# A mixture of experts' last sum: rows stored by token, one more choice on TensorE, shared tiles moved behind the experts, and a first wait for two gathers

## The reference

```python
# x: (T=2048, H=256), E=64 experts, M=176, K=6 choices, C=96 places per expert, MS=352
scores = softmax(x @ gate_weight.T)                  # group-limited, then
topk_w, topk_i = top_k(masked scores, 6)
pos  = running count of the choice's expert          # over all tokens and choices
slot = topk_i * C + minimum(pos, C - 1)              # overflow shares the last place
buf[slot] = x[token]                                 # (E, C, H)
out = (silu(buf @ Wg.T) * (buf @ Wu.T)) @ Wd.T       # per expert
y   = sum over k of out[slot[t, k]] * topk_w[t, k]
shared = (silu(x @ Sg.T) * (x @ Su.T)) @ Sd.T
result = residual + y + shared
```

## Time and profile before

| | |
|---|---|
| median of 3 runs | 1515.64 us (1514.18 to 1516.43) |
| profiled execution | 1511.05 us |
| its span | 1509.4 us |
| mean granted TensorE clock | 0.963 |
| busy: PE / DVE / ACT / POOL | 1376.7 / 1053.4 / 820.4 / 356.5 us |
| DMA moved | 215.08 MB |

### The profile page before, as it was taken

The page is one execution under the profiler, slowest core; times in us unless marked ns, Lnnn a source line. Parts: engine busy times, 40 slices in busy tenths (PEclk is TensorE's granted clock), DMA queues, the critical chain, the costliest instruction groups (busy, mean ns, idle before and its releaser), DMA issues. The chain is left out here.

```text
span 1509.4 us, 36481 instructions
## 1 busy us (share of the span) xinstructions
PE 1376.7 (91%) x12868; PEld 969.4 (64%) x12869; DVE 1053.4 (70%) x2256; ACT 820.4 (54%) x1701; POOL 356.5 (24%) x782
## 2 busy tenths in 40 slices
PE   5769999998779999999979999999997989899977
PEld 3435455454656777777767677777775945799953
DVE  7866777773878888888831888888887679322228
ACT  2335566565138778777820777877785155122230
POOL 0145656420111011111110111110102000677730
PEclk9969999999889999999999999999999999999985
DMA  3059898850027767676640676666666050799958
GB/s 105 1 140 217 247 250 231 217 125 22 1 81 137 138 135 142 136 139 135 133 77 1 111 138 134 137 133 136 132 135 134 29 167 1 217 280 287 272 158 289
DMA packets 463449, 215.08 MB, mean 142 GB/s; under 512 B 412130, under 2 KB 434496, under 8 KB 463120
## 3 DMA queue, kind: packets, MB, share of 16 engines
q1 hardware_dynamic: 449040, 175.09, 51.6%
q0 software_dynamic: 12000, 36.90, 8.2%
q10 hardware_dynamic: 2336, 2.16, 0.4%
HBM read 81.97 MB, written 31.52 MB: 75 GB/s over the span
## 5 line engine op out<-in xcount | busy, mean ns | idle before, releaser
L1076 PE MATMUL bank<-a_pt,v_part 128*128 128x128 f16 x3456 | 234.2, 219 | 17.3 <-DMA a_pt<-a_ph 12.7
L1139 ACT ACTIVATE a_ph<-a_p,a_rinv 128x1024 f16<-128x1024 f32 (+7 forms) x256 | 198.7, 777 | 80.6 <-POOL a_rinv L1018 75.3
L758 DVE TENSOR_REDUCE a_qh<-bank 128x1 f16<-128x1024 f32 (+7 forms) x256 | 182.3, 755 | 84.3 <-PE bank L648 81.8
L1076 PEld LDWEIGHTS bank<-a_pt,v_part 128*128 128x128 f16 x3456 | 207.6, 98 | 51.1 <-DMA a_pt<-a_ph 10.2
L1147 DVE TENSOR_REDUCE a_negm<-bank 128x1 f32<-128x1024 f32 (+7 forms) x256 | 191.8, 750 | 57.0 <-PE bank L1060 56.8
L1055 PE MATMUL bank<-a_k,a_q 128*128 128x512 f16 (+3 forms) x1152 | 228.6, 326 | 0.2
L746 ACT ACTIVATE a_p<-bank 128x1024 f32<-128x1024 f32 (+7 forms) x256 | 158.1, 649 | 128.3 <-PE bank L703 113.3
L1181 DVE SCALAR_TENSOR_TENSOR a_ph<-a_p,a_rinv,a_ph 128x1024 f16<-128x1024 f32 (+7 forms) x256 | 207.0, 809 | 2.0 <-ACT a_ph L1139 2.0
L1128 ACT ACTIVATE a_p<-bank,a_negm 128x1024 f32<-128x1024 f32 (+7 forms) x256 | 189.3, 739 | 21.7 <-DVE a_negm L1147 21.7
L1018 POOL TENSOR_TENSOR a_rinv<-a_rinv,p_scale 128x1 f32<-128x1 f32 x256 | 48.8, 191 | 613.0 <-DVE a_rinv L1160 612.8
L927 PE MATMUL bank<-xT,wsplit 128*128 128x512 f16 x768 | 186.0, 379 | 4.1 <-PEq L213 1.8
(11 more groups left out here) (223 smaller groups left out, 2216.3 us busy)
## 6 DMA issues: line engine op xcount, KB each, us to landing
wgu<-in_wgu SPq DMA_DIRECT2D x64, 352.0 KB
choice_rows<-zero POOLq DMA_DIRECT2D x24, 512.0 KB, 4.1
c_rows<-choice_rows SPq DMA_DIRECT2D x16, 768.0 KB, 11.2
wsplit<-w_parts POOLq DMA_DIRECT2D x30, 384.0 KB, 4.3
wd<-in_wd SPq DMA_DIRECT2D x64, 176.0 KB
pw_in<-in_wqkv SPq DMA_DIRECT2D x16, 384.0 KB, 4.5
w_parts<-pw_part SPq DMA_DIRECT2D x16, 384.0 KB, 3.9
a_pt<-a_ph SPq DMA_TRANSPOSE x256, 3.3
```

The costliest lines, as they stand in the source:

```text
L758: dve.tensor_reduce(qh[s][:, i, MC:MC + 1], s1_place(t), AX.X, ALU.max, negate=True).then_inc(m_ready, 1)
L1076: ins = eng.matmul(Z_ps[:, cols], g.vs[par][v_][:, k, :], turned[slot][:, a * blocks[j] + k, :], start=(k == 0 and (v_, a) == PARTS[0]), s ...
L1139: eng.activation(parts[slot][:, 0:w_], probs[slot][:, 0:w_], ACT.Copy, scale=rinv[:, p_, jj:jj + 1]).then_inc(p_hi, 1)
```

## The change

Five things change. The result rows are laid out by token (row token * 6 + choice), so that the six rows of one token stand together; `g.dst` and the constant `c_last` follow. `KD` falls from 5 to 4, so TensorE takes two choices of each token (two diagonals, two matmuls) and VectorE four. The shared tiles 8 to 11 are no longer computed ahead of the experts and added by VectorE; their `shared_down` runs on TensorE behind the last expert, into the PSUM places of the first four sums, and the last sum starts with these tiles and accumulates on them. The sum uses eight PSUM places for four. And `turn_pair(0, 0)` waits for a semaphore of its own, `s_two`, which only the first two gathers raise; gathers 2 and 3 are waited for at `turn_pair(1, 2)`.

```diff
-    last = np.where(np.arange(P) == C - 1, OOB, -T).astype(np.float32)[:, None]
+    last = np.where(np.arange(P) == C - 1, OOB, -1).astype(np.float32)[:, None]
...
-KD = 5
+KD = 4
...
-             **{t: (1, t // 2 - 4, t % 2) for t in range(8, 12)}, **{t: (3, t // 2 - 6, t % 2) for t in range(12, 16)}}
-LATE = 8
+             **{t: (1, t // 2 - 6, t % 2) for t in range(12, 16)}}
+LATE, LAST = 8, 12
...
-def shared_down(g, pe, t, hT, t0):
+def shared_down(g, pe, out, t, hT, t0, last=True):
     for m in range(NMS):
         w_ = SM[m][1]
-        ins = pe.matmul(shared_bank(g, t), hT[0:w_, m, (t - t0) * P:(t - t0 + 1) * P], g.sd[0:w_, m, :],
-                        start=(m == 0), stop=(m == NMS - 1))
+        ins = pe.matmul(out, hT[0:w_, m, (t - t0) * P:(t - t0 + 1) * P], g.sd[0:w_, m, :],
+                        start=(m == 0), stop=(last and m == NMS - 1))
...
-            chained(dve.tensor_copy(dtmp[:, 0, :], picked[:, 0, :]))
-            chained(dve.scalar_tensor_tensor(dtmp[:, 0, :], picked[:, 1, :], float(T), dtmp[:, 0, :],
+            chained(dve.tensor_copy(dtmp[:, 0, :], picked[:, 1, :]))
+            chained(dve.scalar_tensor_tensor(dtmp[:, 0, :], picked[:, 0, :], float(K), dtmp[:, 0, :],
...
             for e in range(XB):
-                gather(e)
+                gather(e, s_two if e < 2 else None)
...
-                if s % XG == 0:
-                    pe.wait_ge(s_row[s // XG], p_num * (2 * ROWS_IN // XB) + (ROWS_IN - ROWS_IN * s // XB))
+                if (s % XG == 0 or s == 2) and not (isinstance(p_num, int) and p_num == 0):
+                    two = 32 if s < XG else 0
+                    pe.wait_ge(s_row[s // XG], p_num * (2 * ROWS_IN // XB) + (ROWS_IN - two - ROWS_IN * s // XB))
...
-            for t in range(LATE, NT):
-                if t >= 12 and t % 2 == 0:
-                    pe.wait_ge(s_add, t - 10)
-                shared_down(g, pe, t, g.hL, LATE).then_inc(s_dl, 1)
+            for t in range(LAST, NT):
+                shared_down(g, pe, shared_bank(g, t), t, g.hL, LATE).then_inc(s_dl, 1)
+            pe.wait_ge(s_two, 32)
             turn_pair(0, 0)
             pe.wait_ge(s_add, 12)
             gu(0, 0, 0)
-            pe.wait_ge(s_add, NT)
             pe.wait_ge(s_wov, 2)
...
-            for t in range(NT):
-                if t >= LATE:
-                    dve.wait_ge(s_dl, t // 2 * 2 - LATE + 2)
+            for t in (*range(LATE), *range(LAST, NT)):
+                if t >= LAST:
+                    dve.wait_ge(s_dl, t // 2 * 2 - LAST + 2)
...
-    kv = g.krows.rearrange("(k n p) d -> p n k d", n=NT, p=P)
+    kv = g.krows.rearrange("(n p k) d -> p n k d", n=NT, p=P)
+    order = (*range(LATE, LAST), *range(LATE), *range(LAST, NT))
+    places = [g.bank[b_][:, half, 0:D] for b_ in (3, 0, 1, 2) for half in range(2)]
     def load(sp):
         sp.dma_start(last[:, :], g.lrows).then_inc(s_l, 16)
-        for t in range(NT):
-            if t >= NB:
-                sp.wait_ge(s_xs, t - NB + 1)
-            sp.dma_start(rows[t % NB][:, :, :], kv[:, t, :, :]).then_inc(s_g[t % NB], 16)
+        for i, t in enumerate(order):
+            if i >= NB:
+                sp.wait_ge(s_xs, i - NB + 1)
+            sp.dma_start(rows[i % NB][:, :, :], kv[:, t, :, :]).then_inc(s_g[i % NB], 16)
     def matmul(pe):
+        for i in range(LAST - LATE):
+            shared_down(g, pe, places[i], order[i], g.hL, LATE, last=False)
         pe.wait_ge(s_l, 16)
-        for t in range(NT):
-            if t >= 4:
-                pe.wait_ge(s_xs, t - 3)
-            ps = g.bank[t % 4][:, 0, 0:D]
-            pe.matmul(ps, g.wovT[:, t * P:(t + 1) * P], last[:, :], start=True, stop=False)
+        for i, t in enumerate(order):
+            if i >= 8:
+                pe.wait_ge(s_xs, i - 7)
+            ps = places[i % 8]
+            pe.matmul(ps, g.wovT[:, t * P:(t + 1) * P], last[:, :], start=(i >= LAST - LATE), stop=False)
...
```

More of the change, by code:

```diff
@@ L1824, in _ @@
                 for t in (2 * k - 4, 2 * k - 3):
-                    shared_down(g, pe, t, hT, 0)
+                    shared_down(g, pe, shared_bank(g, t), t, hT, 0)
                 pick(k)
@@ L1944, in experts @@
     s_scat = [g.sem(f"x_scatter{i}") for i in range(NR)]
-    s_free = g.sem("x_out_free")
+    s_free, s_two = g.sem("x_out_free"), g.sem("x_first_two")
     s_dl, s_add, s_wov, s_wt, s_we = [g.sem(f"r_{n}") for n in
@@ L1973, in _, with gather @@
         def _(pool):
-            def gather(e):
+            def gather(e, landed=None):
                 pool.indirect_dma_start(out=rows[e % XB // XG][:, e % XG, :], out_offset=None, in_=g.xrows,
                                         in_offset=bass.IndirectOffsetOnAxis(ap=g.src[:, e:e + 1], axis=0),
-                                        bounds_check=T - 1, oob_is_err=False).then_inc(s_row[e % XB // XG], 16)
+                                        bounds_check=T - 1, oob_is_err=False).then_inc(
+                                            landed or s_row[e % XB // XG], 16)
             for e in range(XB):
-                gather(e)
+                gather(e, s_two if e < 2 else None)
             for e in range(E):
@@ L2181, in matmul @@
     def matmul(pe):
+        for i in range(LAST - LATE):
+            shared_down(g, pe, places[i], order[i], g.hL, LATE, last=False)
         pe.wait_ge(s_l, 16)
-        for t in range(NT):
-            if t >= 4:
-                pe.wait_ge(s_xs, t - 3)
-            ps = g.bank[t % 4][:, 0, 0:D]
-            pe.matmul(ps, g.wovT[:, t * P:(t + 1) * P], last[:, :], start=True, stop=False)
-            pe.wait_ge(s_g[t % NB], 16 * (t // NB + 1))
-            pe.wait_ge(s_dg, t + 1)
+        for i, t in enumerate(order):
[3 more added lines that the diff above has]
+            pe.matmul(ps, g.wovT[:, t * P:(t + 1) * P], last[:, :], start=(i >= LAST - LATE), stop=False)
+            pe.wait_ge(s_g[i % NB], 16 * (i // NB + 1))
+            pe.wait_ge(s_dg, i + 1)
@@ L2191, in matmul @@
             for k in range(KD, K):
-                ins = pe.matmul(ps, g.diag[:, t, k - KD, :], rows[t % NB][:, k, :], start=False, stop=(k == K - 1))
+                ins = pe.matmul(ps, g.diag[:, t, k - KD, :], rows[i % NB][:, k, :], start=False, stop=(k == K - 1))
             ins.then_inc(s_mm, 1)
     def weigh(dve):
-        for tiles in ((0,), *((t, t + 1) for t in range(1, NT - 1, 2)), (NT - 1,)):
-            for t in tiles:
-                dve.wait_ge(s_g[t % NB], 16 * (t // NB + 1))
+        for places_ in ((0,), *((i, i + 1) for i in range(1, NT - 1, 2)), (NT - 1,)):
+            for i in places_:
+                dve.wait_ge(s_g[i % NB], 16 * (i // NB + 1))
@@ L2200, in weigh @@
             for k in range(KD):
-                for j, t in enumerate(tiles):
+                for j, i in enumerate(places_):
+                    t = order[i]
                     if k:
-                        dve.wait_ge(s_acc, KD * tiles[0] + len(tiles) * (k - 1) + j + 1)
-                    dve.scalar_tensor_tensor(g.x[:, t, :], rows[t % NB][:, k, :], g.wk[:, t, k:k + 1],
+                        dve.wait_ge(s_acc, KD * places_[0] + len(places_) * (k - 1) + j + 1)
+                    dve.scalar_tensor_tensor(g.x[:, t, :], rows[i % NB][:, k, :], g.wk[:, t, k:k + 1],
@@ L2205, in weigh @@
                                              g.x[:, t, :], ALU.mult, ALU.add).then_inc(s_acc, 1)
[L2206 to L2209, removed]
+            for j, i in enumerate(places_):
+                t = order[i]
+                dve.wait_ge(s_acc, KD * places_[0] + len(places_) * (KD - 1) + j + 1)
+                dve.wait_ge(s_mm, i + 1)
+                dve.tensor_tensor(g.x[:, t, :], places[i % 8], g.x[:, t, :], ALU.add).then_inc(s_xs, 1)
@@ L2211, in store @@
     def store(act):
-        for t in range(NT):
+        for t in order:
             for k in range(KD, K):
@@ L2215, in store @@
             ins.then_inc(s_dg, 1)
-        for t in range(NT):
-            act.wait_ge(s_xs, t + 1)
+        for i, t in enumerate(order):
+            act.wait_ge(s_xs, i + 1)
             act.dma_start(ov[:, t, :], g.x[:, t, :]).then_inc(s_st, 16)
```

## The result

The change made the kernel slower: 1520.29 us (median of 11 runs, 1518.94 to 1522.18) against 1515.97 (11 runs, 1514.18 to 1518.68), a ratio of 1.0028 [1.0018, 1.0037], so 4.3 us. The forecast was 1509.6; rival 1, which gave 1520.8, is what happened. The profiled execution took 1520.36 us.

A forecast was written before the change was run, and what follows sets the result against it. Bounds taken: gather waits in the head, TensorE in the expert loop, DMA loads in the last sum. Head -1.2, VectorE -1.3, DMA -3.5 make -6.0 us: median 1509.6, own range 1507.0 to 1512.5, full range 1507.0 to 1520.5.

The forecast's parts named there:

- rival 1: Last sum: TensorE stays at the low clock and becomes the bound, +5.2 us, a median of 1520.8; chance 0.25.
- Last sum, TensorE: Last sum: 3.15 us a tile at the low clock, not hidden; the clock returns within some tiles, lost time caught up.
- Head: First turn to expert loop: release 2.3 us earlier, low clock after a new hole costs 1.1, net -1.2 us.
- Behind the experts: After the experts: moved shared tiles, 5.3 us, fit TensorE's 6.06 us hole; ScalarE's diagonals ready in time; cost nothing.
- VectorE: End of the last sum: four multiply-adds a tile for five, -1.3 us.
- DMA: Last sum: choice rows load faster in 6 KB runs, -3.5 us, of 0 to -3.8.

The follow-up runs named there:

- Full rows: The changed kernel with the overflow matmuls padded with zeros from 64 to 128 rows, no hole filled: 1507.51 us.
- the head filled: The changed kernel with nine unread matmuls in TensorE's hole ahead of the first turn's wait for two gathers: 1515.8 us.
- fill: The changed kernel with eight unread matmuls in TensorE's hole before the first rows of the last sum: 1507.17 us.
- the hoisted overflow matmuls: The changed kernel with the overflow matmuls of the first eight tiles run together before the rows land: 1510.04 us.
- full rows with both fills: The changed kernel with overflow matmuls over 128 rows and the holes in head and tail filled by unread matmuls: 1506.49 us.

## Why the prediction was wrong

**The step that failed** is the one headed "Last sum, TensorE", and in it one sentence: "I take it that it returns within some tiles". The prices there were right (3.15 us a tile forecast and measured, the fall of the clock at the start of the stage too); what was open was which of two rows to believe, and I believed the output projection's. The new tail was called nearer to it because of its trains of four with a pair between them. The row that I passed over was the tail's own 1.15 us for a pair, which I used as a price and called one "with its pause", without asking whether the projection has that pause too. Full rows, with the same number of instructions and without it, had the clock back after 3.4 us; after kept the low clock for 47 us. By 13.2 us (51.7 for 38.5) this sentence decided the sign.

**Rival 1** was worked out rightly: its 51.9 us from first rows to the end were 51.7, its 1520.8 a median of 1520.29. Only its chance, 0.25, was too small: of the two rows, the one from the same lines, with the same 64-row operand, was the nearer.

**Head.** Forecast: release 2.3 us earlier, loss at the low clock 1.1, net -1.2. Measured: 2.23, 1.4 and -0.86. The clock fell in the 4.22 us hole for 6.8 us (1300.3 to 1307.1), as the 4.25 us row said. That row's hole was a wait for VectorE, this one is a wait for a DMA. The step stands; the low clock was undersized by 0.3 us, and the head filled says the same (7.29 - 5.85 = 1.4). That 2.23 came so near to 2.3 is in part luck: the same two gathers release the turn 9.05 us behind the shared tiles' start in `fill` and 10.37 with `KD = 5` in after, which is 1.5 to 2.8 us earlier than in before.

**Behind the experts.** Nothing forecast, nothing seen: shared tiles 5.36 us in the gap, ScalarE's 32 diagonals 9.45 us, ready before their rows.

**VectorE.** -1.3 forecast for the end; `fill` shows 0.8 + 0.5.

**DMA.** -3.5 forecast, and this term was mis-sized: the loads came 5.8 (`fill`) to 6.6 us (after) sooner, at 420 GB/s for the 396 that I had drawn through two rates. By the estimate from the Trainium skill (DMA: Bandwidth & Descriptors, "Why small descriptors are slow") 2.6 us were to be had (35.6 x 2.5/35 gives 2.5); the runs gave over twice that, and the measurement decides. After could not show it in its time, since TensorE set the end.

**At the full clock** the forecast would have been near: 1509.6 against 1507.2 (`fill`), 2.4 us too high and inside the range that stood beside it. In its profile the miss is the loads: from the first landing to the last 32.1 us for 37.9, 5.8 us less for the 3.5 forecast. VectorE ends 4.2 us behind the last landing (1499.5 against 1495.3) for 5.4 in before, so there the 1.3 us came out as 1.2.

## What to carry to other kernels

Before work is moved to an engine that runs at a low clock while it has little to do, price it at the low clock as well, and if that no longer fits under the bound, plan what brings the clock back: here the added work alone did not, and the same work with full rows did. Of two rows that disagree take the one with the same operands and tile shapes; a pair that takes longer than twice a single instruction can hide a pause, and that belongs to the argument. And when one layout change shifts the bound from the DMA to a compute engine, try the parts alone and together: here the layout is worth 0.43% without the rest, and `KD = 4` costs 0.39% alone in before, while at the full clock it shortens the last sum from 41.3 to 38.5 us.

## What the hardware showed that I had not expected

**A busy record and a low clock.** TensorE stood at 0.50 for 47.4 us while shown busy all of them, and at 1.00 for 27.8 us while shown busy 20.22 of them (full rows). The Trainium skill (TensorE: Matmul & The Clock Gate, "What's actually happening") has sustained activity release the clock; by the records of after that didn't happen, though 0.54 us of each 3.15 in them may be the pauses above.

**The same hole, another clock.** In an attention stage that both kernels share, the holes that end near 768.7 us are alike (2.91 us, 2.99 in after). Before kept 1.00 there; the same stretch of after:

```profile
768.10:774.70 6.60, 5.92 (x54) 5.64 (x54) 0.67 (x2) 0.01 (x1) 0.00 (x0) 0.50 0.61 115
```

Ahead of it the same matmuls of the two profiles start 0.08 us apart (760.86 in before, 760.94 in after); behind it, the next large train of L936 starts at 830.64 in before and 833.47 in after. So 2.8 of the 4.08 us by which the late shared tiles start later arise in this part, which the change doesn't touch. Holes near 2.9 us are followed by the low clock in one execution and not in another, while the unfilled ones ahead of the first turn, 2.6 to 4.9 us long, were followed by it in all six profiles that had one, and those of 1.3 and 1.4 us in neither. The hole of 2.3 us ahead of the late shared tiles, which all twelve profiles have, was followed by it in three: the two gathers alone, the hoisted overflow matmuls, and full rows with both fills. The runs of before beside the experiments went from 1510.2 to 1520.1 us, which is why a stage counted from its own start says more here than a single time.
